# Row pieces of an attention loop spread over twelve passes, and two sets of GpSimd additions moved from one stage to the next

## The reference

```python
def _L1_xattn_ref(x, y, wq, wk, wv, wo, ln_gamma, ln_beta):
    def bit_linear(x, w):            # x / rms(x), rounded to 8-bit steps row by row
        xn = _rms_norm(x)
        xq = _ste(xn, _act_quant(xn))
        ...
        return jnp.einsum('bni,oi->bno', xq, wq)
    q = bit_linear(x, wq); k = bit_linear(y, wk); v = bit_linear(y, wv)
    ...
    attn = jax.nn.softmax(scores, axis=-1)
    out = jnp.einsum('bhgns,bhsd->bhgnd', attn, v)
    out = (out - mu) * jax.lax.rsqrt(var + LN_EPS) * ln_gamma + ln_beta
    return bit_linear(out, wo)
x = x + _L1_xattn_ref(_layernorm(x), ctx_1024, ...)
# _L1_attn_ref: n = _layernorm(x); y = selective scan over n
#   r = y @ out_proj_w.T + out_proj_b + n
#   x = x + (r - mu) * lax.rsqrt(var + LN_EPS) * ln_gamma + ln_beta
# _L1_ffn_ref: eight dense experts of gelu(x w1 + b1) w2 + b2, one gate
```

## Time and profile before

| What | us |
|---|---|
| median of 3 runs | 1782.86 |
| lowest and highest | 1780.49, 1787.54 |
| the profiled execution | 1780.72 |
| its span, first to last instruction | 1778.9 |
| PE busy, share of the span | 1352.1, 76% |
| DVE busy | 1285.0, 72% |
| ACT busy | 1023.1, 58% |
| POOL busy | 764.4, 43% |

### The profile page before, as it was taken

The page is one execution under the profiler, slowest core; times in us unless marked ns, Lnnn a source line. Parts: engine busy times, 40 slices in busy tenths (PEclk is TensorE's granted clock), DMA queues, the critical chain, the costliest instruction groups (busy, mean ns, idle before and its releaser), DMA issues. The chain is left out here.

```text
span 1778.9 us, 33549 instructions
## 1 busy us (share of the span) xinstructions
PE 1352.1 (76%) x12580; PEld 769.0 (43%) x12580; DVE 1285.0 (72%) x2324; ACT 1023.1 (58%) x1851; POOL 764.4 (43%) x808
## 2 busy tenths in 40 slices
PE   6999347988679887778845837344788789799898
PEld 4544123655544355555532312002345445355566
DVE  3698899961368675777667739999999899985200
ACT  2676335433444476777653447433798798885553
POOL 2355000000232434434414016656788788877443
PEclk9999668999779988788967868556899899899999
DMA  6496200000145576687512358997564465560000
GB/s 261 160 356 264 80 0 0 1 1 0 67 148 166 173 136 121 116 145 127 82 34 89 99 134 207 248 222 199 139 164 115 120 163 130 125 148 8 1 13 13
DMA packets 152516, 212.37 MB, mean 119 GB/s; under 512 B 107199, under 2 KB 112255, under 8 KB 139296
## 3 DMA queue, kind: packets, MB, share of 16 engines
q1 hardware_dynamic: 152356, 210.23, 46.1%
HBM read 155.37 MB, written 31.75 MB: 105 GB/s over the span
## 5 line engine op out<-in xcount | busy, mean ns | idle before, releaser
L2782 POOL TENSOR_TENSOR mf_st<-mf_st,mf_c_rep 128x1024 f32<-128x1024 f32 x128 | 301.3, 2354 | 202.5 <-DVE mf_st L2850 202.5
L2850 DVE TENSOR_TENSOR_SCAN mf_st<-mf_dA,mf_u_ps 128x512 f32<-128x512 f32 x256 | 309.9, 1211 | 0.0
L2673 PE MATMUL mf_y_ps<-mf_st,c_consts 128*32 128x512 f32 x512 | 130.0, 735 | 135.0 <-POOL mf_st L2782 99.1
L2961 ACT ACTIVATE mf_dA<-c_dt,c_neg_a 128x496 f32<-128x496 f32 x256 | 163.8, 699 | 69.1 <-DVE mf_st L2850 68.2
L2844 DVE TENSOR_TENSOR mf_u_ps<-mf_st,mf_b_ps 128x512 f32<-128x512 f32 x256 | 177.7, 694 | 21.5 <-DMA mf_st<-xs 10.6
L2805 POOL TENSOR_TENSOR mf_hid<-mf_g,mf_hid 128x512 f16<-128x512 f32 x128 | 148.3, 1159 | 95.9 <-ACT mf_g L2978 95.9
L2975 ACT ACTIVATE mf_hid<-mf_eh,c_vecs 128x512 f16<-128x512 f32 x128 | 87.9, 687 | 122.4 <-PE mf_eh L2724 121.9
L2724 PE MATMUL mf_eh<-mf_parts,mf_w 128*128 128x512 f16 x480 | 125.0, 399 | 19.6 <-POOL mf_parts L2801 18.0
L259 POOL TENSOR_TENSOR c_parts<-mg_ln_hT,c_parts 128x512 f16<-128x512 f32 x8 | 9.0, 1156 | 302.6 <-ACT c_parts L250 302.5
L2111 DVE TENSOR_REDUCE t_mx<-t_s_ps 128x2 f32<-128x514 f32 x128 | 87.8, 687 | 56.9 <-PE t_s_ps L1997 56.8
L2057 ACT ACTIVATE t_p<-t_s_ps,t_mx 128x257 f32<-128x257 f32 x256 | 107.2, 476 | 20.2 <-DVE t_mx L2111 18.2
(11 more groups left out here) (510 smaller groups left out, 2998.7 us busy)
## 6 DMA issues: line engine op xcount, KB each, us to landing
mf_st<-xs SPq DMA_DIRECT2D x64, 1024.0 KB, 7.2
a_ctx_t<-in_ctx_t SPq DMA_DIRECT2D x16, 1024.0 KB, 9.0
a_ctx_n<-in_ctx_n SPq DMA_DIRECT2D x16, 1024.0 KB, 8.0
cqs<-a_whole_rows SPq DMA_DIRECT2D x16, 512.0 KB, 6.7
mo_raw<-in_l_w SPq DMA_DIRECT2D x16, 512.0 KB, 4.0
ws<-mo_split SPq DMA_DIRECT2D x32, 256.0 KB, 2.6
c_cq<-cqs SPq DMA_DIRECT2D x16, 512.0 KB, 5.1
mf_w<-ws SPq DMA_DIRECT2D x20, 256.0 KB, 11.6
```

The lines of the kernel that those rows point to most:

```text
L2673: m = e.matmul(y_ps[T * j:T * j + T, :], c.pick[:, gg, :], st[u % RING][:, j, :], start=(gg == 0), stop=(gg == 3))
L2782: e.tensor_tensor(half(u, h), half(u, h), over(c_rep[u // UNITS % 2][:, :], [P, 2, BT], 1), ALU.mult).then_inc(hcs("done"), 1)
L2850: e.tensor_tensor_scan(st[u % RING][:, j, :], dA[:, n % AHEAD, :], u_ps[j % 2][:, :], 0.0, ALU.mult, ALU.add).then_inc(hs("done"), 1)
L2961: e.activation(by_batch(dA[:, n % AHEAD, :])[:, :, 1:], dt, ACT.Exp, scale=c.neg_a[:, at:at + 1]).then_inc(dAs("done"), 1)
```

## The change

In the attention loop, squares and second root become two pieces, and so do the quantisation (its scale, and its integers) and the norm of the attended rows (gamma, and the rest). The pieces of a group are put in other passes:

| piece | queries before | now | attended before | now |
|---|---|---|---|---|
| squares / second root (ACT) | 3 / 3 | 3 / 4 | 3 / 3 | 4 / 5 |
| gamma / norm (DVE) | - / 2 | - / 2 | 2 / 2 | 2 / 3 |
| scale / integers (DVE) | 4 / 4 | 5 / 6 | 4 / 4 | 6 / 7 |
| transpose (SP) | 5 | 7 | 5 | 8 |
| matmuls and drains | 7, 8 | 8, 9 | 7, 8 | 9, 10 |
| rounding (ACT), rest (POOL) | 9 | 10 | | |
| transposes of the parts (SP) | 10, 11 | 11, 12 | | |

The last pieces of the third attended group fall behind pass 63, where they stand ahead of the loop's old tail. In the inner stage GpSimd has nothing to do any more: the normalised rows go to DRAM as they are. The bias is now added in the last stage, in position 0 of each block (`bias`), and the residual waits for it; beta is added to `c_x` in slots 3, 6, 9 and 12 (`shift`).

```diff
--- before.py
+++ after.py
...
+    quantise_scale(e, own, rt, r, factor, i)
+    quantise_ints(e, own, ints, r)
+
+
+def quantise_scale(e, own, rt, r, factor, i):
+
     e.tensor_reduce(r.amax[:, :], r.xn[:, :, :], AX.X, ALU.max, apply_absolute_value=True).then_inc(*own())
...
     e.wait_ge(*own.now())
+
+
+def quantise_ints(e, own, ints, r):
+
     for k in range(KT_):
...
 def row_rt(e, squares, rt, r, junk, i, c):
+    row_squares(e, squares, r, junk)
+    row_root(e, squares, rt, r, i, c)
+
+
+def row_squares(e, squares, r, junk):
     for k in range(KT_):
         e.activation(junk[:, k, :], r.xn[:, k, :], ACT.Square, accum_out=r.ss[:, k:k + 1]).then_inc(squares("done"), 1)
+
+
+def row_root(e, squares, rt, r, i, c):
     e.wait_ge(*squares.at("done", i))
...
         block = ctx.enter_context(nc.Block())
-        GROUPS = B // BPT
+        GROUPS, PAST = B // BPT, 4
...
-            return ([("q", query(b, 7 + h), h) for h in range(2) if query(b, 7 + h) > 0] +
-                    [("x", project_out(b, 7 + h), h) for h in range(2) if project_out(b, 7 + h) >= 0])
+            return ([("q", query(b, 8 + h), h) for h in range(2) if query(b, 8 + h) > 0] +
+                    [("x", project_out(b, 9 + h), h) for h in range(2) if project_out(b, 9 + h) >= 0])
         ring = []
-        for b in range(B + 2):
+        for b in range(B + PAST):
             ring += extras(b)
...
                     fetch(b // BPT + 2)
-                if query(b, 5):
-                    turn_queries(query(b, 5))
+                if query(b, 7):
+                    turn_queries(query(b, 7))
                 for x in range(2):
-                    if query(b, 10 + x):
-                        send(query(b, 10 + x), x)
-                if project_out(b, 5) >= 0:
-                    turn_attended(project_out(b, 5))
+                    if query(b, 11 + x):
+                        send(query(b, 11 + x), x)
+                if project_out(b, 8) >= 0:
+                    turn_attended(project_out(b, 8))
                 if b % BPT == 2 and b > BPT:
...
                     fetch_last(b // BB + 1)
+            for b in range(B, B + PAST):
+                if project_out(b, 8) >= 0:
+                    turn_attended(project_out(b, 8))
             for w in range(BPT):
...
                     split(b + LEAD)
-                if query(b, 9):
-                    low_query(query(b, 9))
+                if query(b, 10):
+                    low_query(query(b, 10))
...
-            def query_rt(i):
+            def query_squares(i):
                 e.wait_ge(*q_normed.at("done", i - 1))
-                row_rt(e, q_squares, q_rt, qr, junk, i - 1, c)
-
-            def attended_rt(i):
+                row_squares(e, q_squares, qr, junk)
+
+            def attended_squares(i):
                 e.wait_ge(*x_normed.at("done", i))
-                row_rt(e, x_squares, x_rt, xr, xjunk, i, c)
+                row_squares(e, x_squares, xr, xjunk)
...
                 if query(b, 3):
-                    query_rt(query(b, 3))
-                if query(b, 9):
-                    round_query(query(b, 9))
+                    query_squares(query(b, 3))
+                if query(b, 4):
+                    row_root(e, q_squares, q_rt, qr, query(b, 4) - 1, c)
+                if query(b, 10):
+                    round_query(query(b, 10))
                 if project_out(b, 1) >= 0:
                     row_std(e, x_var, x_std, xr, project_out(b, 1), c)
-                if project_out(b, 3) >= 0:
-                    attended_rt(project_out(b, 3))
+                if project_out(b, 4) >= 0:
+                    attended_squares(project_out(b, 4))
+                if project_out(b, 5) >= 0:
+                    row_root(e, x_squares, x_rt, xr, project_out(b, 5), c)
             row_std(e, x_var, x_std, xr, BLOCKS - 1, c)
-            attended_rt(BLOCKS - 1)
+            attended_squares(BLOCKS - 1)
+            row_root(e, x_squares, x_rt, xr, BLOCKS - 1, c)
...
+            def query_scale(i):
+                e.wait_ge(*q_normed.at("done", i - 1))
+                quantise_scale(e, own, q_rt, qr, c.wf[:, 0:1], i - 1)
+
             def query_ints(i):
-                e.wait_ge(*q_normed.at("done", i - 1))
                 if i > 1:
                     e.wait_ge(q_turned, (i - 1) * 16)
-                quantise(e, own, q_rt, q_ints, qr, c.wf[:, 0:1], i - 1)
+                quantise_ints(e, own, q_ints, qr)
...
-            def attended_norm(i):
+            def attended_gain(i):
                 r = xr
...
                                            ALU.subtract, ALU.mult).then_inc(*own())
+
+            def attended_norm(i):
+                r = xr
                 e.wait_ge(*own.now())
...
+            def attended_scale(i):
+                e.wait_ge(*x_normed.at("done", i))
+                quantise_scale(e, own, x_rt, xr, c.wf[:, 3:4], i)
+
             def attended_ints(i):
-                e.wait_ge(*x_normed.at("done", i))
                 if i:
                     e.wait_ge(x_turned, i * 16)
-                quantise(e, own, x_rt, x_ints, xr, c.wf[:, 3:4], i)
+                quantise_ints(e, own, x_ints, xr)
...
                     query_norm(query(b, 2))
-                if query(b, 4):
-                    query_ints(query(b, 4))
+                if query(b, 5):
+                    query_scale(query(b, 5))
+                if query(b, 6):
+                    query_ints(query(b, 6))
                 if project_out(b, 0) >= 0:
...
                 if project_out(b, 2) >= 0:
-                    attended_norm(project_out(b, 2))
-                if project_out(b, 4) >= 0:
-                    attended_ints(project_out(b, 4))
+                    attended_gain(project_out(b, 2))
+                if project_out(b, 3) >= 0:
+                    attended_norm(project_out(b, 3))
+                if project_out(b, 6) >= 0:
+                    attended_scale(project_out(b, 6))
+                if project_out(b, 7) >= 0:
+                    attended_ints(project_out(b, 7))
+            for b in range(B, B + PAST):
+                if project_out(b, 7) >= 0:
+                    attended_ints(project_out(b, 7))
             combine(GROUPS - 1)
...
             attended_stats(BLOCKS - 1)
+            attended_gain(BLOCKS - 1)
             attended_norm(BLOCKS - 1)
+            attended_scale(BLOCKS - 1)
             attended_ints(BLOCKS - 1)
...
             e.dma_start(c.w_z, c.d["l1_w_in"][:, :, DI:2 * DI]).then_inc(w_z_in, 16)
+            e.wait_ge(*N.at("norm", 0))
             for i in range(BLOCKS):
-                e.wait_ge(*resid.at("done", i))
-                e.dma_start(c.d["xns"][i], res[:, i * KT_:(i + 1) * KT_, :]).then_inc(xn_out, 16)
+                e.dma_start(c.d["xns"][i], n.xn[:, i * KT_:(i + 1) * KT_, :]).then_inc(xn_out, 16)
             for i in range(BLOCKS):
...
                 e.wait_ge(ssm_out[u], BLOCKS // 2 * 16)
-
-        @block.gpsimd
-        def _(e):
-            resid.start(e)
-            shifted.start(e)
-            for i in range(BLOCKS):
-                at = slice(i * KT_, (i + 1) * KT_)
-                e.wait_ge(*N.at("norm", 0))
-                e.tensor_tensor(res[:, at, :], n.xn[:, at, :], over(c.row["out_b"], [P, KT_, C], 1), ALU.add).then_inc(resid("done"), 1)
-            for i in range(BLOCKS):
-                at = slice(i * KT_, (i + 1) * KT_)
-                e.tensor_tensor(c.X[:, at, :], c.X[:, at, :], over(c.row["m_beta"], [P, KT_, C], 1), ALU.add).then_inc(shifted("done"), 1)
...
         GATES = (BLOCKS - 1) * DC
+        SHIFTS = (3, 6, 9, 12)
...
+            def bias(b):
+                e.wait_ge(r_in, (b + 1) * 16)
+                e.tensor_tensor(r[:, :, :], r[:, :, :], over(c.row["out_b"], [P, KT_, C], 1), ALU.add).then_inc(biased("done"), 1)
+
+            def shift(b):
+                e.tensor_tensor(c.X[:, rows(b), :], c.X[:, rows(b), :], over(c.row["m_beta"], [P, KT_, C], 1),
+                                ALU.add).then_inc(*pown())
+
             def gain(b):
...
-            for each in (hcs, gated, affine, rests, los):
+            for each in (hcs, gated, biased, affine, rests, los):
                 each.start(e)
...
                 steps = hiddens(s)
+                if s in SHIFTS:
+                    shift(SHIFTS.index(s))
                 if s < N:
                     weigh(s, 0)
+                if p == 0:
+                    bias(b)
                 if p == 2:
...
             def residual(b, kk):
-                e.wait_ge(r_in, (b + 1) * 16)
+                e.wait_ge(*biased.at("done", b))
                 e.wait_ge(*outs.at("done", 2 * b + kk))
```

More of the change, by code:

```diff
@@ L2256, in l1_inner @@
         ssm = [sb(f"ssm{u}", [NR, BT]) for u in range(2)]
-        res = sb("res", [P, TILES, C])
         lg, na, ez, wz, lz, dz, mz, step = (sb(f"dt_{k}", [P, TILES]) for k in
@@ L2272, in l1_inner @@
                                   (("x_t", DC), ("z_t", DC), ("rows_t", 1), ("lg_t", 1)))
```

(3 more changed lines are left out.)

## The result

| What | before | changed |
|---|---|---|
| median of the runs (4 each), us | 1785.20 | 1806.16 |
| lowest and highest | 1780.49, 1789.89 | 1798.82, 1817.05 |
| the profiled execution | 1780.72 | 1802.43 |
| its span | 1778.9 | 1800.6 |
| its mean granted clock | 0.856 | 0.839 |

The ratio is 1.0106, 95% interval 1.0073 to 1.0140: slower by some 19 us, where I had forecast 5 us faster with a range up to 1791. The prediction was wrong.

The account below looks back on a forecast made before the run. Short waits bound the attention loop, GpSimd's additions slow the inner stage, VectorE sets the last stage's end. Inner -6.9, last 0, loop +1.8, tail 0 make -5.1 us: 1775.6 profiled, 1777.8 as median, range 1764 to 1791.

Parts of the forecast that it names:

- the sum of the loop: Attention loop: root -11.0, integers' transpose +9.8, keys +11.1 and time given back -8.1 make +1.8 us.
- the wait gets shorter, TensorE keeps its clock: Attention loop: reason given for the root's gain of 2.2 us a group, TensorE waiting less for ScalarE.
- Inner stage: Inner stage: without GpSimd's additions VectorE's taps run undisturbed and the x-projection starts earlier, -6.9 us.
- Last stage: Last stage: GpSimd's arriving additions fit its idle times and leave the scans alone, cost 0.
- rival C: Last stage: by the port rule each bias addition meets VectorE, +9.4 us, 1787; chance 0.05.
- Root: Attention loop: second root a pass later shortens TensorE's wait for ScalarE, -2.2 us in each of five groups, -11.0.
- The integers' transpose: Attention loop: transpose nearer its matmuls makes new TensorE waits, 2.4 us per query group, 1.3 per attended group, +9.8.
- Keys: Attention loop: GpSimd's rest and one more transpose between key transposes delay the keys, +5.3 and twice +2.9, +11.1 us.
- Given back: Attention loop: passes after the three key waits (1.6 us each) and three query waits (1.1 each) run shorter, -8.1.
- Attended pieces: Attention loop, two attended groups: -2.2 us each from the root's move, +1.3 each from the nearer transpose.
- Tail: Behind the loop: third attended group's savings of 1.3 and 2.2 us against 3.5 more on SyncE's queue, sum 0.
- B: Attention loop: SyncE's queue between key transposes decides, nothing given back, root worth 1 us a group; +13.8, 1797; chance 0.13.

Follow-up runs that it names:

- kernel 2: Attention pieces of queries and attended rows in their new passes, inner and last stage as before; ratio 1.0115 against the kernel before.
- kernel 3: Only the queries' pieces in their new passes, attended pieces and both later stages as before; ratio 1.0144 against the kernel before.
- kernel 5: As kernel 3, with the queries' second root put back in pass 3; ratio 1.0137 against the kernel before.
- kernel 11: As kernel 8, with GpSimd's additions moved to the last stage; ratio 0.9940 against the kernel before, the fastest.
- kernel 14: As kernel 11, with the queries' second root put back in pass 3; ratio 0.9997 against the kernel before.
- kernel 13: As kernel 9, with the queries' rounding and rest a pass later too, in 11; ratio 1.0068 against the kernel before.
- kernel 8: As kernel 3, queries one pass later from the matmuls on (9, 10; rounding and rest 11; parts' transposes 12, 13); ratio 0.9997 against the kernel before.
- kernel 9: As kernel 3, with the transposes of the queries' parts a pass later, in 12 and 13; ratio 1.0099 against the kernel before.
- kernel 4: Only the attended rows' pieces in their new passes, queries and both later stages as before; ratio 1.0011 against the kernel before.
- kernel 6: As kernel 3, with rounding, rest and the parts' transposes back in passes 9, 9, 10 and 11; ratio 1.0035 against the kernel before.

## Why the prediction was wrong

The step that failed is the sum of the loop, +1.8 us where kernel 2 measured +20.5, and in it above all the sentence that "the wait gets shorter, TensorE keeps its clock". TensorE didn't: the loop's clock fell from 0.84 to 0.77, and its matmuls took 18.6 us longer behind the new waits, a cost for which the sum has no term. Step by step:

- **Inner stage, -6.9:** right, -8.1 in the profile (104.6 to 96.5). **Last stage, 0:** right. GpSimd gains 18.5 us of work there and VectorE's busy time is unchanged (555.0, 554.6), so rival C is out.
- **Root, -11.0:** no gain can be seen in kernel 3 (kernel 5). The long wait is gone, but passes 4 to 7 took 19.1 us and before 19.2, since the shorter waits that replaced it left passes 6 and 7 at 0.50 and 0.63 of the clock. In the first group that shorter wait is one without a releaser:

```profile
654.39 0.51 PE L2042 MATMUL t_o_ps<-t_v,t_pt 128*32 128x17 f32 x20 [2.25 <-issue]
```

  Such an idle time of 1.3 to 2.9 us stands near pass 5, 21 or 37 in ten of the twelve profiles with the queries' root in pass 4, and in none of the five with it in pass 3. In kernel 11 the queries' moves alone are worth 10 us (kernel 14).
- **The integers' transpose, +9.8 (7.2 of it for queries):** right in place, and its waits sum to 6.2 us; mis-sized in price. I priced the wait and not the slow pass behind it. The last step from kernel 13 to 8 measures 12.7 ± 6 us.
- **Keys, +11.1:** right in place, and near in size: passes 12 to 15, 28 to 31 and 44 to 47 took 5.6, 2.4 and 5.4 us longer than before. It is two waits. The first, for the keys of pass 11, which GpSimd's rest delays, grew from 3.59 to 4.72 us, by 1.1 where I had 2.1. The second, 2.47 us at pass 15, is new and comes from the queue, where the distance of the two key transposes grew from 10.0 us to 12.6 (I had 13.2):

```profile
688.66 1.23 SPq L1877 DMA_TRANSPOSE t_kT<-t_parts  x1
...
701.23 1.24 SPq L1877 DMA_TRANSPOSE t_kT<-t_parts  x1
```

  What the queue's part costs in time isn't settled: kernel 9 takes it away and gives back 8 ± 8 us, with another wait in its place.
- **Not in the sum:** rounding in the pass of the attended root, 5.5 ± 7 us by kernel 13's time, and some 4 us in each of passes 27 and 43 by its profile. I priced each set of pieces by itself, and the table of lags had it: 16+10 = 25+1.
- **Given back, -8.1:** fell. It rested on one short pass of 2.2 us behind a long one, and passes behind the new waits are long: 5.90 us in pass 9, 5.05 in pass 13.
- **Attended pieces:** my terms for them were -4.4 and +2.6, and kernel 4 measured +2 (-2.5 to +6.4). **Tail, 0:** right as a sum, though not where I put it. The tail is 3.9 us longer, but passes 57 to 61 are 20.4 us and before 24.5; each of the four kernels with the attended pieces' new passes shows both (tails of 33.9 to 35.0 us against 30.1 to 31.5 in all the others, and 20.4 to 21.6 us against 23.4 to 26.0 for the passes).

Of the rivals, B (the queue decides, 1797) was nearest: it counted neither a return nor a full root. It was too low because queue and keys are only a part. Its chance of 0.13 was the more serious error: passes 12 to 15 and 44 to 47, two of its three places, took 5.6 and 5.4 us longer than before, over the 4 us from which it decides; the third, 28 to 31, took 2.4. Its other premises held as well: no return, and little from the root.

## What to carry to other kernels

A wait of TensorE costs its length and also the matmuls behind it at the lower clock; price both from a pass that the trace shows at each level. A piece that moves in a periodic schedule must be held against every other periodic set, on each engine and queue, and not only against its neighbours in its own set. And spreading work pays only while the distance from each transfer to its reader stays: the same split pieces cost 26 us in kernel 3 and nothing in kernel 8, where all from the matmuls on stands one pass later.

## What the runs showed of the hardware

- After a wait of 2 to 3 us TensorE mostly ran a whole pass at its lower level (in the changed kernel passes 6, 9 and 38, at 0.50 and 0.51, behind 2.25, 2.78 and 2.28 us): the same 109 matmuls take 3.0 us at a clock of 1.00 and 5.0 to 5.1 at 0.50.
- GpSimd's eight additions cost VectorE nothing in the last stage, but its subtraction of the parts stretched four instructions of VectorE with two SBUF inputs to 5.44 and 4.55 us, where they take 1.8 undisturbed. Size doesn't protect: in kernel 6 an instruction of 128x4 elements took 2.02 us beside it, and 0.16 in before. The Trainium skill (SBUF — State Buffer, Who interferes with whom) has such instructions exclude each other; the trace agrees, and it is the start of one beside the other that decides, so that a shift of one pass brings the stretch or takes it away.
- TensorE has idle times of up to 4.4 us for which the profile names no releaser, and they move from kernel to kernel: 4.37 us in pass 9 of kernel 4. The traces point to the fetching of its own instructions. The page of its profile lists a DMA queue of the kind "instruction" with 101 packets of 16384 bytes:

```profile
q8 instruction: 101, 1.65, 0.4%
```

  In the loops of the 17 profiles TensorE has 60 idle times of over 1.5 us without a releaser, and every one ends 2.0 to 3.8 us (median 2.4) behind the start of a packet of this queue; the one of 2.25 us in pass 5 of the changed kernel ends at 654.39, its packet started at 651.9 and the packet ahead of it at 644.9. The 210 other waits of this length, for engines and transfers, end anywhere from 0.1 to 12.9 us behind such a packet. That is a link in time; no run varied it, and why a packet comes late isn't shown.
